# Attention on split float16 rows a batch ahead, and a swap of two stores

## The reference

```
def _L1_attn_ref(x, Wq, bq, Wk, bk, Wv, bv, Wf, bf):
    Q = _rope(x @ Wq.T + bq)
    K = _rope(x @ Wk.T + bk)
    V = x @ Wv.T + bv
    A = jnp.einsum('btd,bsd->bts', Q, K) / jnp.sqrt(jnp.float32(C))
    A = jnp.where(causal, A, -jnp.inf)
    A = jax.nn.softmax(A, axis=-1)
    out = jnp.einsum('bts,bsd->btd', A, V)
    return out @ Wf.T + bf
...
h = h + _L0_ffn_ref(_layernorm(h, axis=-1), ...)
h = h + _L1_attn_ref(_layernorm(h, axis=-1), ...)
h = h + _L1_ffn_ref(_layernorm(h, axis=-1), ...)
```

## Time and profile before

| | us |
|---|---|
| median of three runs | 773.11 |
| the profiled execution | 775.75 |
| its span, first to last instruction | 773.4 |
| PE busy | 708.4 (92%) |
| DVE busy | 447.8 (58%) |
| ACT busy | 365.3 (47%) |
| POOL busy | 271.0 (35%) |

### The profile page before, as it was taken

The page is one execution under the profiler, slowest core; times in us unless marked ns, Lnnn a source line. Parts: engine busy times, 40 slices in busy tenths (PEclk is TensorE's granted clock), DMA queues, the critical chain, the costliest instruction groups (busy, mean ns, idle before and its releaser), DMA issues.

```text
span 773.4 us, 18105 instructions
## 1 busy us (share of the span) xinstructions
PE 708.4 (92%) x6013; PEld 620.4 (80%) x6014; DVE 447.8 (58%) x1222; ACT 365.3 (47%) x865; POOL 271.0 (35%) x251
## 2 busy tenths in 40 slices
PE   5989964899999999989899998799999999999981
PEld 5869954789888887667788987788888888888871
DVE  4898786334444344437797777845454545455540
ACT  5899453343333433343667666243434343344430
POOL 2301200222233223214355440225556555564431
PEclk9999997899999999999999999799999999999996
DMA  9996998114122211127841469212233233323235
GB/s 260 232 191 73 129 164 268 45 29 119 28 32 41 36 22 28 21 45 202 170 48 11 53 78 294 68 37 42 42 55 55 41 45 50 55 44 45 36 36 153
DMA packets 42181, 66.20 MB, mean 86 GB/s; under 512 B 3648, under 2 KB 29232, under 8 KB 41584
## 3 DMA queue, kind: packets, MB, share of 16 engines
q0 software_dynamic: 22272, 39.19, 33.6%
q1 hardware_dynamic: 19664, 25.93, 10.7%
q10 hardware_dynamic: 192, 0.38, 0.2%
HBM read 65.80 MB, written 23.35 MB: 115 GB/s over the span
## 4 chain that ended last, share of the span: by engine, by line
PE 76%; DVE 12%; DMA 4%; ACT 4%; issue 2%; POOL 1%; POOLq 0%; SPq 0%; DVEq 0%
PE PS L1148 16%; PE PS L1161 15%; PE PS L855 14%; PE PS L892 8%; PE PS L1507 3%; PE PS L2443 3%; PE PS L870 3%; PE PS L2457 2%; DMA xs<-Y 2%; PE PS L1534 1%; ACT Y L2161 1%; PE PS L1457 1%; PE PS L1133 1%; DMA X<-in_w_dram 1%; PE PS L1515 1%
## 5 line engine op out<-in xcount | busy, mean ns | idle before, releaser
L1161 PE MATMUL PS<-X 128*128 x720 | 125.7, 273 | 1.9 <-ACT X L1230 1.9
L1148 PE MATMUL PS<-X 128*128 128x256 f16 (+1 forms) x768 | 122.7, 265 | 0.9 <-DVE X L1250 0.5
L1319 POOL DMA_INDIRECT sum<-X,dest x45 | 89.1, 1980 | 96.1 <-ACT X L1230 81.0
L1220 ACT ACTIVATE X<-PS,X 128x256 f32<-128x256 f32 (+1 forms) x192 | 72.8, 463 | 103.3 <-PE PS L1148 103.3
L855 PE MATMUL PS<-Y,X 128*128 128x256 f16 x960 | 109.0, 274 | 0.0
L855 PEld LDWEIGHTS PS<-Y,X 128*128 x960 | 94.4, 98 | 11.2
L1148 PE MATMUL PS<-X,Y 128*128 128x256 f16 (+1 forms) x384 | 100.2, 264 | 0.0
L1161 PE MATMUL PS<-Y,X 128*128 x360 | 98.2, 273 | 0.0
L1148 PEld LDWEIGHTS PS<-X 128*128 x768 | 71.6, 97 | 11.0 <-issue 1.6
L1161 PEld LDWEIGHTS PS<-X 128*128 128x128 f16 x720 | 70.4, 98 | 10.6 <-issue 2.6
L1119 POOL DMA_INDIRECT sum<-Y,dest x24 | 38.7, 1614 | 111.5 <-DVE Y L1052 107.9
(11 more groups left out here) (401 smaller groups left out, 1339.5 us busy)
## 6 DMA issues: line engine op xcount, KB each, us to landing
X<-in_w_dram POOLq DMA_DIRECT2D x16, 1024.0 KB, 13.7
sum<-h SPq DMA_DIRECT2D x2, 2048.0 KB, 17.0
Y<-in_w_dram POOLq DMA_DIRECT2D x4, 1024.0 KB, 11.6
xs<-Y SPq DMA_DIRECT2D x2, 1040.0 KB, 6.9
xs<-Y SPq DMA_DIRECT2D x2, 1032.0 KB, 12.5
h<-in_txt_dram SPq DMA_DIRECT2D x2, 1024.0 KB, 17.5
Y<-in_patches_dram SPq DMA_DIRECT2D x3, 672.0 KB, 8.4
sum<-h SPq DMA_DIRECT2D x2, 768.0 KB, 15.7
```

What stands on the lines that cost most here:

```text
L1148: ins = nc.tensor.matmul(PS[:, 2 * s + c // 2, (c % 2) * T1:(c % 2) * T1 + tokens], part[:, off:off + P], x_[:, slot, k, 0:tokens], start= ...
L1161: ins = nc.tensor.matmul(PS[:, 4 + a, 0:D], h_[:, s, c, a * P:(a + 1) * P], part[:, off:off + D], start=(s == 0 and c == 0 and n == 0), st ...
L1220: ins = nc.scalar.activation(hh1[:, s, c, 0:tokens], PS[:, 2 * s + c // 2, (c % 2) * T1:(c % 2) * T1 + tokens], ACT.Gelu, bias=bias1[:, sl ...
L1319: nc.gpsimd.indirect_dma_start(out=sum1, out_offset=bass.IndirectOffsetOnAxis(ap=dest[:, i:i + 1], axis=0), in_=y1buf[:, u % 2, i - first_ ...
```

## The change

It has two parts that don't depend on each other.

Six split instructions have come ahead of the first `rope`, and two between it and the weight transfers, which follow here as before. The diff, cut to its core:

```
+NEGATED1 = (0, 0, 1, 1, 1, 1, 1, 2, 1, 1, 2, 1, 1, 2, 1, 0)
+ADD_IN = (6, 9, 12)
...
         def sp_rest(sp):
-            for t, n in ((0, BATCH), (BATCH, IT)):
-                sp.wait_ge(h_added, t + n)
-                sp.dma_start(sum0[t * P:(t + n) * P].rearrange("(t p) n -> p t n", p=P), h[:, t:t + n, :])\
-                    .then_inc(sum_based, 16)
             sp.wait_ge(pay_ready, 1)
...
+            sp.wait_ge(x_in[0], 32)
+            for t, n in ((0, BATCH), (BATCH, IT)):
+                sp.wait_ge(h_added, t + n)
+                sp.dma_start(sum0[t * P:(t + n) * P].rearrange("(t p) n -> p t n", p=P), h[:, t:t + n, :])\
+                    .then_inc(sum_based, 16)
...
-                for k in range(KC):
-                    ins = nc.tensor.transpose(PS[:, 7, k * P:(k + 1) * P], xnF[:, slot, k * P:(k + 1) * P], k_ident)
+                for q in range(2 * KC):
+                    ins = nc.tensor.transpose(turned2[:, q * P:(q + 1) * P], xn2[:, slot, q // KC, q % KC * P:(q % KC + 1) * P],
+                                              ident2)
...
-                            ins = nc.tensor.matmul(PS[:, bank, m * SEQ:(m + 1) * SEQ], w_[:, k, m * P:(m + 1) * P],
-                                                   xTb[:, slot, k, :], start=(k == 0), stop=(k == KC - 1))
+                            for n, (wh, xq) in enumerate(((0, k), (0, KC + k), (1, k))):
+                                ins = nc.tensor.matmul(PS[:, bank, m * SEQ:(m + 1) * SEQ], w_[:, wh, k, m * P:(m + 1) * P],
+                                                       xTb[:, slot, xq, :], start=(k == 0 and n == 0),
+                                                       stop=(k == KC - 1 and n == 2))
...
-                if b < BATCH - 2:
-                    text(b + 2, slot)
                 if b == BATCH - 1:
...
+                if b < BATCH - 2:
+                    text(b + 2, slot)
             heads(pe, batch)
...
-                for n in range(b + 1 if b else 0, min(b + 2, W1W // CW)):
+                for n in range(sum(NEGATED1[0:b]), sum(NEGATED1[0:b + 1])):
...
+            act.wait_ge(attn_loaded, 96)
+            nc.scalar.activation(wqk2[:, 0, :], wqk, ACT.Copy).then_inc(wqk_parts, 1)
+            nc.scalar.activation(ident2, k_ident, ACT.Copy).then_inc(wqk_parts, 1)
...
-                if b < BATCH - 2:
-                    norm(b + 2, 2 if b < 2 else 3 if b < 6 else 4)
+                if b < BATCH - 3:
+                    norm(b + 3, 2 if b < 1 else 3 if b < 5 else 4)
                 normalise_p(b, slot)
-                if b < BATCH - 2:
-                    text(b + 2, slot)
-                else:
+                if b >= BATCH - 2:
                     negate(b)
                 copy_pt(b)
...
                 if b < BATCH - 2:
+                    text(b + 2, slot)
                     negate(b)
...
+            def split_text(b):
+
+                pool.wait_ge(xn_ready, NF + b + 1)
+                if b >= 2:
+                    pool.wait_ge(xn_tr, AHEAD + b - 1)
+                nc.gpsimd.tensor_copy(xn2[:, b % 2, 0, :], xnF[:, b % 2, :]).then_inc(own_rounded, 1)
+                pool.wait_ge(own_rounded, b + 1 + (b > 0))
+                nc.gpsimd.tensor_tensor(xn2[:, b % 2, 1, :], xnF[:, b % 2, :], xn2[:, b % 2, 0, :], ALU.subtract)\
+                    .then_inc(xn_split, 1)
...
+            split_text(0)
             image(0)
+            pool.wait_ge(prep_copied, 4)
+            split_values()
+            split_text(1)
             image(1)
             rope(0)
-            pool.wait_ge(prep_copied, 4)
             bias(0)
             bias(1)
+            split_text(2)
...
+                if b < BATCH - 3:
+                    split_text(b + 3)
+                if b < BATCH - 2:
                     bias(b + 2)
...
-                if b and b % (W1N // CW) == 0:
-                    add(b * CW // W1N - 1)
+                if b in ADD_IN:
+                    add(ADD_IN.index(b))
...
+                chain.link(nc.vector.tensor_scalar(xnF[:, 2 + n, :], h[:, t, :], mv[:, t, 0:1], rstd[:, t:t + 1],
+                                                   ALU.subtract, ALU.mult))
+                chain.link(nc.vector.tensor_copy(xi2[:, n % 2, 0, :], xnF[:, 2 + n, :]))
+                nc.vector.tensor_tensor(xi2[:, n % 2, 1, :], xnF[:, 2 + n, :], xi2[:, n % 2, 0, :], ALU.subtract)\
+                    .then_inc(xi_ready, 1)
...
+                if b == 0:
+                    moments_back(4, MIDDLE[0] - 3, MIDDLE, 6 + len(MIDDLE))
                 if b == 1:
-                    moments_back(4, MIDDLE[0] - 3, MIDDLE, 6 + len(MIDDLE))
                     norm_image(2)
-                if 2 <= b < 5:
-                    stats_of(LATE[b - 2::3])
+                if 1 <= b < 4:
+                    stats_of(LATE[b - 1::3])
+                if b == 4:
+                    moments_back(8, NT - 8, LATE, NT)
                 if b == 5:
-                    moments_back(8, NT - 8, LATE, NT)
                     norm_image(3)
```

More of the change, by code:

```diff
@@ L327, in build @@
         xnF = rx.take([IT + 2, D])
-        xTi = rx.take([KC, IT, P])
-        xTb = rx.take([2, KC, SEQ])
+        xTi = rx.take([2 * KC, IT, P], F16)
+        xTb = rx.take([2, 2 * KC, SEQ], F16)
         qkT = rx.take([2, 2, KC, SEQ])
@@ L343, in build @@
         rsum = rx.take([2, 2])
+        xn2, xi2 = rx.take([2, 2, D], F16), rx.take([2, 2, D], F16)
+        wqk2 = stage[:, 1, :].bitcast(F16).rearrange("p (h n) -> p h n", h=2)
+        wq2, wk2 = (wqk2[:, :, i * KC * D:(i + 1) * KC * D].rearrange("p h (k n) -> p h k n", k=KC) for i in range(2))
+        wvx2 = wqk.bitcast(F16)[:, 0:2 * KC * PAYV].rearrange("p (h k n) -> p h k n", h=2, k=KC)
+        ident2 = stage[:, 0, CW - P // 2:CW].bitcast(F16)
+        turned2 = PS[:, 7, :].bitcast(F16)
         rg = Region(X, XE)
@@ L396, in build @@
         d_moved = sem("d_moved")
-        w0_cast = [sem(f"w0_cast{i}") for i in range(W0C // CAST)]
+        w0_cast = [sem(f"w0_cast{i}") for i in range(4)]
         dve_negated = sem("dve_negated")
@@ L493, in build @@
         p_exp = sem("p_exp")
+        own_rounded = sem("own_rounded")
+        xn_split = sem("xn_split")
+        wqk_parts = sem("wqk_parts")
+        wvx_split = sem("wvx_split")
         p_normed = sem("p_normed")
@@ L1514, in text_values @@
                 for k in range(KC):
-                    ins = nc.tensor.matmul(PS[:, 2, 0:PAYV], xTb[:, slot, k, IMG:SEQ], wvx[:, k, :],
-                                           start=(k == 0), stop=(k == KC - 1))
+                    for n, (xq, wh) in enumerate(((k, 0), (k, 1), (KC + k, 0))):
+                        ins = nc.tensor.matmul(PS[:, 2, 0:PAYV], xTb[:, slot, xq, IMG:SEQ], wvx2[:, wh, k, :],
+                                               start=(k == 0 and n == 0), stop=(k == KC - 1 and n == 2))
                 ins.then_inc(v_psum, 1)
@@ L1525, in image_values @@
                 for k in range(KC):
-                    ins = nc.tensor.matmul(PS[:, 5, 0:PAYV], xTi[:, k, n, :], wvx[:, k, :], start=(k == 0), stop=(k == KC - 1))
+                    for j, (xq, wh) in enumerate(((k, 0), (k, 1), (KC + k, 0))):
+                        ins = nc.tensor.matmul(PS[:, 5, 0:PAYV], xTi[:, xq, n, :], wvx2[:, wh, k, :],
+                                               start=(k == 0 and j == 0), stop=(k == KC - 1 and j == 2))
                 ins.then_inc(vi_psum, 1)
@@ L1636, in image @@
                 act.wait_ge(xi_tr, n + 1)
-                nc.scalar.activation(xTi[:, :, n, :], PS[:, IMAGE_BANK[n], 0:KC * P].rearrange("p (k r) -> p k r", k=KC),
-                                     ACT.Copy).then_inc(xTi_copied, 1)
+                nc.scalar.activation(xTi[:, :, n, :], PS[:, IMAGE_BANK[n], :].bitcast(F16)[:, 0:2 * KC * P]
+                                     .rearrange("p (k r) -> p k r", k=2 * KC), ACT.Copy).then_inc(xTi_copied, 1)
             def beside(n):
-                nc.scalar.activation(xTi[:, :, n, :], PS[:, 7, BESIDE:BESIDE + KC * P].rearrange("p (k r) -> p k r", k=KC),
-                                     ACT.Copy).then_inc(xTi_copied, 1)
+                nc.scalar.activation(xTi[:, :, n, :], turned2[:, 2 * BESIDE:2 * BESIDE + 2 * KC * P]
+                                     .rearrange("p (k r) -> p k r", k=2 * KC), ACT.Copy).then_inc(xTi_copied, 1)
             def text(b, slot):
```

43 lines of the change are left out of this document (27 added, 16 removed).

## The result

The changed kernel takes 769.91 us (median of six runs, 769.18 to 771.37), the one before 773.14 beside it: a ratio of 0.9941 (95% interval 0.9917 to 0.9965). It is faster, as forecast, but by 3 to 5 us and not by 14: the forecast 758.8 is missed, and so is its range. The profiled execution took 770.28, its span 768.5 in place of 773.4.

A forecast was written before the change was run, and what follows sets the result against it. The prediction took layer 0's store wait and, in attention, PE's list alternating with a PE-DVE-POOL loop as bounds. Terms -7.9 - 7.1 - 1.3 + 2.0 = -14.3 took 775.75 to 761.4, as a median 758.8; eight-in-ten range 750.5 to 768.

The forecast's parts named there:

- Layer 0: Ahead of layer 0's experts: normed-row stores land earlier without the residual ahead, PE starts 6.5 earlier and keeps its clock: -7.9.
- Rival B: Layer 0's stores don't gain their 6.5 since weight transfers hold them: -2.5 in place of -7.9, total 764.2; chance 0.09.
- q's half and the plain batches: Attention loop: q's twelve matmuls take 0.88 where its half took 1.24; nine batches not set by DVE take 5.6 each.
- losses: Attention loop: POOL's splits make additions late and ACT's longer copies and double negations delay exponentials: +2.0, from 0 to +6.
- Rival C: Attention loop: weight loads show, q's twelve take 1.24, plain intervals stay at 5.9: total 761.8; chance 0.08.
- Rival D: Attention: POOL becomes the bound with a cast of 0.93, plain batches stay at 5.9: total 770.6; chance 0.08.
- the split's price: POOL in the attention: one text split, a cast of 0.45 and a subtraction of 0.73, costs 1.2.
- The batches that DVE sets: Attention loop: four intervals set by late DVE statistics take 6.4, 5.95, 7.0 and 6.55; 13 batches sum to 76.3, -7.1.
- DVE's length E plus a tail: Attention loop: when statistics make DVE late, the interval is their length E plus 3.04, from maxima to end of k.
- rival E: Attention loop: PE waits about 0.6 in each batch and its clock falls, so the kernel is slower, 786; chance 0.05.
- The attention's start: Start of attention: ACT's wait for weights goes (-5.3), against +0.9, +0.8 and +2.3 from POOL and DVE: -1.3.
- The rule that was weighed: DVE and POOL share ports held for a whole instruction; norm_images of batches 1 and 6 could wait 0.7 each: 1.4.

The follow-up runs named there:

- the swap alone: Kernel before the change, with only SP's five issues reordered so the residual's stores come after the normed rows' stores: 766.08 us, ratio 0.9906.
- the narrow splits: Changed kernel with POOL's cast and subtraction for text rows cut to 2 of 256 columns from batch 3 on: 767.72 us, ratio 0.9921.
- all edits: Changed kernel with wq/wk subtraction and image splits on POOL, newt/old instructions and double negations moved, POOL's batch 4 wait, PE fillers: 762.79 us, ratio 0.9854.
- the attention alone: Changed kernel with the residual's stores ahead of the normed rows again, so only the attention is changed: 776.92 us, ratio 1.0041.
- the moved subtraction: Changed kernel with the subtraction that splits wq and wk done by POOL after its last scatter, not by DVE: 767.48 us, ratio 0.9911.

## Why the prediction was wrong, step by step

*Layer 0: right.* Forecast -7.9, measured -7.4 at the second unit's products (139.69 for 147.12); the swap alone took 7 us off the whole. The stores took 5.3 to 5.9 (6.2 forecast). The gathered rows are in at 131.27 (131.05 forecast), and the transposes start at 131.90, since what is late next is PE's own list, two matmuls and fillers behind DVE's work; the clock (1.00 from there on) and the shorter wait between transposes and products gave back 1.8 in place of 1.4. That the residual's later stores cost nothing held. Rival B falls.

*q's half and the plain batches: right.* 0.89 for 0.88 forecast. The nine plain intervals take 53.3, for 50.4 and 2.0 of losses. Rival C falls with the 0.89. The Trainium skill, "TensorE: Matmul & The Clock Gate", section "Back-to-back issue gap", gives some 81 ns a pair at 128 columns; this trace disagrees, with 74 ns a pair at 165 columns. Rival D falls with the narrow splits, and the split's price was right: a cast is 0.40 and a subtraction 0.67, 1.1 for 1.2.

*The batches that DVE sets: this step failed.* Four intervals hold 4.6 of the 5.5 that the loop misses. In numbers:

| interval (scores to scores) | forecast | changed kernel | all edits |
|---|---|---|---|
| 2 to 3 (`norm_image`, four statistics) | 6.4 | 7.54 | 6.37 |
| 4 to 5 (`add_image`, three statistics) | 5.95 | 5.85 | 5.84 |
| 5 to 6 (moments) | 7.0 | 9.66 | 7.39 |
| 7 to 8 (`add_image`, `norm_image`) | 6.55 | 7.47 | 6.44 |
| the nine others, with losses | 52.4 | 53.3 | 52.2 |
| sum | 78.3 | 83.8 | 78.2 |

In the main the mechanism was the right one, DVE's length E plus a tail, but the E were built of durations from a trace in which POOL had no splits to do beside them, and this change puts POOL's splits right there. The moments are 3.9 for 2.96, `norm_image` 1.7 to 1.9 for 1.0 (1.1 where POOL is idle). So E, from `add_text` to the maxima, is 3.97 for 3.4, 4.90 for 3.95 and 4.43 for 3.5 in the three long intervals: 2.4 of the 4.6. The tail on DVE was right (3.03 to 3.04), but in two of the three it isn't what ends the interval. The late maxima make p late too, and PE's list behind p's transposes, with the image's products in it, ends after POOL's addition for k. In the interval of 7.54 that addition is done at 377.23, but PE comes to the scores (377.84) only behind

```profile
377.62 0.39 PE L1505 MATMUL PS<-stage,X 128*128 128x128 f16 x4
```

This second path, which the prediction left out, costs 0.5 there and 0.3 behind the moments (8.27 at full clock, for 4.90 + 3.04 = 7.94). The remaining 1.4 is the clock. With the collisions and double negations out of the way and the image splits on POOL the loop takes what was forecast, but by other edits, so that the two sums agree is luck and bears nothing out. Of the 9.66, 0.9 is the collision and 1.4 the clock, which is rival E at one place instead of in every batch: the granted clock is 0.85 here.

*The attention's start: failed too.* Forecast -1.3, measured +2.4. To the first scores it takes 3.7 longer in place of 0.9: 1.2 is the scatter held by DVE's subtraction, which the prediction let fall into a wait and looked at from DVE's side alone; 1.3 is the second Newton iteration beside `split_values` (two instructions of 0.59 and 1.05 in place of 0.19); 1.6 are the two longer `norm_image`s (0.8 each, 0.6 forecast), of which 0.4 comes back, as PE's list no longer ends behind POOL's addition. POOL's second text split, also ahead of the first `rope`, ends with `image` at 354.62, as DVE's q does (354.55), and costs next to nothing. Then batch 1 is 0.5 late for 0.8, and the next interval shortens by 1.9 for 3.0: the moments of batch 0 are held as well, 3.8 where they take 2.85 when POOL waits for them. ACT's wait for weights is gone, as forecast.

*The rule that was weighed.* A row showed a short DVE instruction held beside POOL's addition. I priced this at 1.4 and for `norm_image` alone. It is the larger part of the miss: at the moments of batches 4 and 0, the Newton iteration at the start, the two `norm_image`s and the scatter it is 0.9 + 0.9 + 1.3 + 1.2 + 1.2 = 5.5, of the 9.4 by which the change of the spans misses the forecast (4.9 for 14.3). For the moments and the scatter an edit takes the wait away and so shows the cause; for the Newton iteration and `norm_image` it is read from the durations alone. The Trainium skill, "SBUF — State Buffer", section "SBUF: two separate sides", says that DVE and GpSimd share a pair of ports as an exclusive lock, that DVE takes part in this in a two-port mode or with two inputs in SBUF, and that whoever starts first blocks the other for its whole instruction. The traces agree that each can hold the other (0.65 for 0.17 on DVE, 2.60 for 1.55 on POOL).

## What to carry to other kernels

When a change puts small instructions on two engines that can hold each other, look at who runs beside whom at the places where one of them is already late, and don't carry a duration over from a trace in which the other engine was idle. Work that is off the critical path can be told to wait there: one wait on POOL gave back 0.9 in the interval behind it and cost nothing in the next ones. And when two independent edits come together, time each alone: here one gives 7 us and hides that the other costs 3.

## What was not expected of the hardware

Not every DVE instruction is held by POOL. Three statistics in a row take 1.06 beside POOL's subtraction, as much as without it (1.39 for four):

```profile
384.43 0.67 POOL L1799 TENSOR_TENSOR X<-X 128x256 f16<-128x256 f32 x1
384.54 1.06 DVE L1860 BATCH_NORM_STATS2 stats<-h 128x6 f32<-128x256 f32 x3
```

DVE's instructions that read PSUM keep their 0.37 beside POOL's additions for q and k. What was held are scalar operations, casts and two-input operations on SBUF, also the shortest (128x14 values). And behind one and the same wait of PE (2.46 in batch 5) the granted clock fell in the profiles of three of these kernels (the interval is 9.66, 9.35 and 9.89: the changed one, the attention alone, the moved subtraction) and stayed at 1.00 in two others (8.27, 8.26); what decides it stays open.
